# Routing in a mixture-of-experts stage: token weights formed later, column comparisons split per tile, placing matmuls dealt out between wide ones

## The reference

```
scores = sigmoid(x @ gate_w.T) + bias
topk_w, topk_idx = top_k(scores, 4)
topk_w = topk_w / (sum(topk_w) + 1e-20)
out = sum over the 4 chosen experts e of topk_w * (silu(x @ Wg[e].T) * (x @ Wu[e].T)) @ Wd[e].T
out = out + (silu(x @ Sg.T) * (x @ Su.T)) @ Sd.T      # the shared expert
x = layernorm(x + out)
```

## Time and profile before

| | us |
|---|---|
| median of 3 runs | 1754.04 (1752.56 to 1755.8) |
| profiled execution, its own time | 1757.54 |
| span of its trace | 1755.7 |
| PE busy | 1689.7 |
| DVE busy | 1267.1 |
| ACT busy | 919.4 |
| POOL busy | 958.2 |

### The profile page before, as it was taken

The page is one execution under the profiler, slowest core; times in us unless marked ns, Lnnn a source line. Parts: engine busy times, 40 slices in busy tenths (PEclk is TensorE's granted clock), DMA queues, the critical chain, the costliest instruction groups (busy, mean ns, idle before and its releaser), DMA issues. The chain is left out here.

```text
span 1755.7 us, 39041 instructions
## 1 busy us (share of the span) xinstructions
PE 1689.7 (96%) x15461; PEld 964.6 (55%) x15461; DVE 1267.1 (72%) x2051; ACT 919.4 (52%) x1518; POOL 958.2 (55%) x875
## 2 busy tenths in 40 slices
PE   7899998899999999999999999999899999999997
PEld 4666664455555555555555555555455555455553
DVE  6778776778888888888888888888785444344445
ACT  6776674656464645455555545565643333233334
POOL 5556664556464636465555555464634555455544
PEclk9999999899999999999999999999999999999999
DMA  5431223112212314122222122131266778877658
GB/s 163 133 86 39 74 62 80 61 58 88 70 64 72 109 43 142 46 100 93 72 73 97 37 97 73 37 109 37 77 226 216 145 146 224 241 190 151 116 97 299
DMA packets 88897, 190.68 MB, mean 109 GB/s; under 512 B 14800, under 2 KB 33744, under 8 KB 86672
## 3 DMA queue, kind: packets, MB, share of 16 engines
q1 hardware_dynamic: 65232, 130.72, 22.3%
q0 software_dynamic: 22912, 57.32, 16.0%
q10 hardware_dynamic: 576, 0.14, 0.0%
HBM read 124.95 MB, written 63.21 MB: 107 GB/s over the span
## 5 line engine op out<-in xcount | busy, mean ns | idle before, releaser
L1136 POOL TENSOR_TENSOR xa_sc<-xa_sc,xa_rs 128x1024 f32<-128x1024 f32 x32 | 60.8, 1901 | 375.4 <-DVE xa_rs L1396 375.4
L1125 POOL TENSOR_TENSOR xa_xs<-xa_xs,sn 128x512 f32<-128x512 f32 x160 | 233.7, 1460 | 46.3 <-ACT xa_xs L1177 46.3
L288 PE MATMUL bank<-xhl,front_h 128*128 128x512 f16 x640 | 244.4, 382 | 11.3 <-DVE front_l L670 10.0
L289 PE MATMUL bank<-xhl,front_h 128*128 128x512 f16 x640 | 244.3, 382 | 0.0
L290 PE MATMUL bank<-xhl,front_l 128*128 128x512 f16 x640 | 244.1, 381 | 0.0
L1130 POOL TENSOR_TENSOR xa_rr<-xa_x,xa_xs 128x512 f32<-128x512 f32 x160 | 232.2, 1451 | 12.7 <-DVE xa_x L1287 0.2
L2042 POOL DMA_INDIRECT scratch_y<-raw_front,moe_to x79 | 125.3, 1585 | 149.5 <-DVE mo_zl L2096 121.5
L288 PE MATMUL bank<-out_h,xa_oh 128*128 128x512 f16 x512 | 194.8, 381 | 10.2 <-DVE xa_ol L1269 8.0
L289 PE MATMUL bank<-out_l,xa_oh 128*128 128x512 f16 x512 | 194.7, 380 | 0.0
L290 PE MATMUL bank<-out_h,xa_ol 128*128 128x512 f16 x512 | 194.5, 380 | 0.0
L1176 ACT ACTIVATE xa_xs<-bank 64x512 f32<-64x512 f32 x160 | 95.0, 593 | 139.3 <-PE bank L290 124.4
(11 more groups left out here) (320 smaller groups left out, 4668.8 us busy)
## 6 DMA issues: line engine op xcount, KB each, us to landing
xa_rawc<-in_ew SPq DMA_DIRECT2D x32, 768.0 KB, 5.4
moe_ring<-scratch_w SPq DMA_DIRECT2D x16, 1536.0 KB
scratch_w<-xa_chunk_h SPq DMA_DIRECT2D x32, 384.0 KB, 2.3
scratch_w<-xa_chunk_l SPq DMA_DIRECT2D x32, 384.0 KB, 3.3
raw_front<-in_xwq SPq DMA_DIRECT2D x8, 1024.0 KB, 7.9
raw_out<-in_xwo SPq DMA_DIRECT2D x8, 1024.0 KB, 5.3
scratch_y<-acc SPq DMA_DIRECT2D x6, 1024.0 KB, 7.8
acc<-in_x POOLq DMA_DIRECT2D x4, 1024.0 KB, 7.2
```

Source lines behind the costliest of these rows:

```text
L288: pe.matmul(out_ap, ah, bh, start=start and m == 0, stop=False)
L289: pe.matmul(out_ap, ah, bl, start=False, stop=False)
L1125: PO.mark(pool.tensor_tensor(xr, xr, sn[:, :].rearrange("p (a s) -> p a s", a=1) .to_broadcast([P, QT // S, S]), ALU.mult), f"sm{r}", st)
L1136: PO.mark(pool.tensor_tensor(s4, s4, rs[:, :, :].rearrange("p h (t a) -> p (h t) a", a=1) .to_broadcast([P, 16, S]), ALU.mult), "nm", st)
```

## The change

It does four things.

**Column comparisons.** `hit` and its semaphore are gone. Where DVE made a group's `at_col` with two operations over 128x664 (a comparison with the column numbers, then a product with the token numbers), it now makes it with eight operations over 128x83, each a comparison and a product in one, whose two scalars are read per partition (`colf[:, j, t:t+1]` and `m.tok_no[:, t:t+1]`). `at_col` is laid out [P, 8, 83] in place of [P, 83, 8], so that a placing matmul streams 83 adjacent elements; `at_row` keeps its layout, its 128 weights 16 bytes apart. The float16 copy `col` goes, a float16 copy `ioh` of the column numbers is made ahead of the scores.

**Tokens' weights.** The four operations that make `m.w4` move from ahead of the counts to behind `locate(0, 1, 2, 3)`.

**Placing matmuls.** 24 of groups 0 to 3 follow a wide matmul of gu1.1 each and the other 8 stand behind it; 12 of groups 4 to 7 follow a wide matmul of y0.2 and y0.3 each, and the other 20 stand behind. y0.0 and y0.1 move ahead of gu1.1.

**Low part.** zl of the quarter q = 1 moves from POOL to DVE, behind "list", and PE waits for it there.

```diff
-            at_row, at_col = ([b(f"{w}{n}", [P, c, NR], F16) for n in range(NB)] for w, c in (("at_row", P), ("at_col", COLS)))
-            hit, s_hit = [b(f"hit{n}", [P, COLS, NR], F16) for n in range(2)], sem("ro_hit")
+            at_row, at_col = ([b(f"{w}{n}", shape, F16) for n in range(NB)] for w, shape in (("at_row", [P, P, NR]), ("at_col", [P, NR, COLS])))
+            ioh = b("ioh", [P, P], F16)
...
             PE = Timeline(sem("ro_pe"), [], 0,
-                          ["logits"] + quad("gu", 0, IB) + ["counts"] + quad("gu", 1, IB) + several("place", *range(4)) + ["y0.0"]
-                          + several("place", *range(4, 8)) + ["owners", "y0.1", "y0.2", "y0.3", "y1.0", "y1.1", "turn0", "y1.2", "turn1", "y1.3"])
+                          ["logits"] + quad("gu", 0, IB) + ["counts", "gu1.0", "y0.0", "y0.1", "place0", "place1", "gu1.1", "place2", "place3", "y0.2", "place4",
+                                                                "y0.3"] + several("place", *range(5, 8)) + ["owners", "y1.0", "y1.1", "turn0", "y1.2", "turn1", "y1.3"])
...
-                          ["down", "chosen"] + quad("z", 0, IB) + ["w4", "slots"] + several("at", *range(4)) + quad("z", 1, IB)
-                          + several("at", *range(4, 8)) + ["own", "list", "tables", "to", "xl0", "xl1", "ws0", "ws1"])
+                          ["down", "chosen"] + quad("z", 0, IB) + ["slots"] + several("at", *range(4)) + ["w4"] + quad("z", 1, IB)
+                          + several("at", *range(4, 8)) + ["own", "list"] + quad("zl", 1, IB) + ["tables", "to", "xl0", "xl1", "ws0", "ws1"])
...
-                        dve.tensor_tensor(hit[g % 2][:, :, :], io8[:, 0:COLS, :], along(col[:, j, ts], COLS), ALU.is_equal).then_inc(s_hit, 1)
                         dve.tensor_tensor(at_row[g % NB][:, :, :], io8[:, :, :], along(row[:, j, ts], P), ALU.is_equal)
-                        dve.wait_ge(s_hit, g + 1)
-                        i = dve.tensor_tensor(at_col[g % NB][:, :, :], hit[g % 2][:, :, :], along(m.tok_no_h[:, ts], COLS), ALU.mult)
+                        for n in range(NR):
+                            t = ts.start + n
+                            i = dve.tensor_scalar(at_col[g % NB][:, n, :], ioh[:, 0:COLS], colf[:, j, t:t + 1], m.tok_no[:, t:t + 1],
+                                                  ALU.is_equal, ALU.mult)
...
                 products(0)
-                then(dve.tensor_reduce(tot[:, :], top8[:, :, 0:TOPK], AX.X, ALU.add))
...
                 wait(dve, PE, "counts")
...
                 locate(0, 1, 2, 3)
+                then(dve.tensor_reduce(tot[:, :], top8[:, :, 0:TOPK], AX.X, ALU.add))
...
                 products(1)
                 locate(4, 5, 6, 7)
...
+                for n in range(IB):
+                    wait(dve, AC, f"zh1.{n}")
+                    DV.mark(dve.tensor_tensor(zl[1][:, n, :], z[:, n, :], zh[1][:, n, :], ALU.subtract), f"zl1.{n}", N0)
...
-                front(1)
-                place_picks(0, 1, 2, 3)
-                back(0, 0)
-                place_picks(4, 5, 6, 7)
+                front(1, 0)
+                back(0, 0, 1)
+                front_with_places(1, 1, range(4))
+                back(0, 2, 3, groups=range(4, 8))
                 wait(pe, DV, "own")
                 PE.mark(pe.matmul(bank[1][0:1, 0:NTILES + 2], own_h[:, :], identh[:, 0:NTILES + 2], start=True, stop=True), "owners", N0)
-                back(0, 1, 2, 3)
                 back(1, 0, 1)
```

More of the change, by code:

```diff
@@ L1879, in logits, with place @@
                     return mm
-                def place_picks(*groups):
-                    for g in groups:
+                def place(g, n):
+                    if n == 0:
                         wait(pe, DV, f"at{g}")
[L1884 to L1888, removed]
+                    j, t = g * NR // NT, (g * NR + n) % NT
+                    mm = pe.matmul(bank[0][:, j * COLS:(j + 1) * COLS], at_row[g % NB][:, :, n], at_col[g % NB][:, n, :],
+                                   start=t == 0, stop=t == NT - 1, skip_group_check=True)
+                    if n == NR - 1:
@@ L1889, in place_picks, with front @@
                         PE.mark(mm, f"place{g}", N0)
-                def front(q, ns=range(IB)):
+                def front(q, n):
                     tok = slice(q * QT, (q + 1) * QT)
[L1893 to L1901, removed]
@@ L1903, in back @@
-                def back(q, *ts):
+                    if q:
+                        wait(pe, DV, f"z{q - 1}.{n}")
+                    for u in range(2):
+                        c = u * FI + n * P
+                        mm = three_pass(pe, bank[2 + 2 * n + u][:, :], [(wf_h[:, k, c:c + P], wf_l[:, k, c:c + P], xh[:, k, tok], xl[:, k, tok])
+                                                                       for k in range(KD)])
+                    PE.mark(mm, f"gu{q}.{n}", N0)
+                def places(groups, first, last):
+                    for m in range(first, min(last, NR * len(groups))):
+                        place(groups[m // NR], m % NR)
@@ new lines, in front_with_places @@
+                def front_with_places(q, n, groups):
+                    wait(pe, DV, f"z{q - 1}.{n}")
+                    tok, m = slice(q * QT, (q + 1) * QT), 0
+                    for u in range(2):
+                        c, o = u * FI + n * P, bank[2 + 2 * n + u]
+                        for k in range(KD):
+                            h, l = wf_h[:, k, c:c + P], wf_l[:, k, c:c + P]
+                            for w, x in ((h, xh), (l, xh), (h, xl)):
+                                mm = pe.matmul(o[:, :], w, x[:, k, tok], start=k == 0 and w is h and x is xh,
+                                               stop=k == KD - 1 and x is xl, skip_group_check=True)
+                                m += 1
+                                if m == 6 * KD:
+                                    PE.mark(mm, f"gu{q}.{n}", N0)
+                                places(groups, m - 1, m)
+                    places(groups, m, 4 * NR)
@@ L1904, in back @@
+                def back(q, *ts, groups=()):
                     if q == 0:
                         wait(pe, DV, "down")
-                    wait(pe, PO, f"zl{q}.1")
+                    wait(pe, DV if q else PO, f"zl{q}.1")
+                    m = 0
                     for t in ts:
```

33 lines of the change are left out of this document (20 added, 13 removed).

## The result

The changed kernel takes 1760.25 us (median of 9 runs, 1758.24 to 1763.82) against 1755.12 (9 runs, 1752.03 to 1757.15) on the same chip: ratio 1.0032, 95% interval 1.0022 to 1.0041, so it is slower by 5.6 us (3.9 to 7.2 at the interval's ends). 4.1 us were forecast.

The account below looks back on a forecast made before the run. The prediction took SP's queue as the bound: the late write delays the fourth load and so turn0 by 4.1 us, added to the median 1754.04 for 1758.1 us. Range 1753.0 to 1761.0, its own 1756.9 to 1760.

Parts of the forecast that it names:

- Price of the new operation: DVE's groups: pitch p of one 83-value operation with two per-partition operands, 0.22 us, a group 2.36 us.
- Start of the groups: DVE behind the counts: the first group starts 1.27 us earlier, at 1315.05 instead of 1316.32.
- The write: SP's queue: the write of the tokens' weights is delayed by max(0, 32p - 2.93), 4.1 us at p = 0.22.
- the fourth load: SP's queue: the fourth expert's weights, behind the write, are issued at 1335.8 instead of 1331.68.
- Rows land with the fourth load.: DMA queues: the first gathered rows land as the fourth load ends, at 1343.2 in the changed kernel.
- Delay of turn0 = delay of the load.: Turning of the first gathered rows: comes 4.1 us later, at 1343.2 against 1339.1, nothing absorbing the delay.
- The later list is hidden; none of PE's order counts.: List about 7 us later, at 1338.5, hidden by the load; PE's 7 us saved in placing turn into waits.
- the 1 us of the forecast: PE before turn0: 12 wide matmuls of 0.216 take it to 1342.2, 1 us ahead of the rows.
- One operand's price: Rival on DVE's pitch: p about 0.16, write delayed 1.2 to 3.1 us, time 1755.3 to 1757.2; chance 0.27.
- free operands: Rival on DVE's pitch: p up to 0.11, delay up to 0.6 us, time 1754 to 1754.7; chance 0.12.
- "Faster": Rival: rows come before the fourth load, turn0 4 to 4.8 us earlier, time about 1749.5; chance 0.08.
- The forecast's other term for PE: PE before turn0: some 8 of 12 wide matmuls at half clock bring it to 1343.9, 0.7 us late.

Follow-up runs that it names:

- a4: Changed kernel with 24 more DVE operations of 83 float16 values behind the last table, results unused; its one time was 1761.61 us.
- a2: Changed kernel, but the write of the tokens' weights on SP's queue waits for at6 instead of w4; ratio to before 1.0047.
- b3: Changed kernel, but SP issues the fourth load only when the first gather's rows have landed; ratio to before 1.0033.
- c2: Kernel before, but SP issues the fourth load right behind the third without waiting for its landing; ratio to before 1.0002.
- a1: Changed kernel, but the write of the tokens' weights waits for the fifth group (at4) instead of w4; ratio to before 1.0031.
- a3: Changed kernel with the three operations per group and the at_col layout of before; ratio to before 1.0016.
- b1: Kernel before with only the changed kernel's column comparisons and at_col layout; ratio to before 1.0041.
- b2: Changed kernel with the weights' four operations back ahead of the counts; ratio to before 1.0042.
- c3: Kernel before, placing matmuls dealt out two behind each wide one of y0.0 to y0.3, fourth load issued right behind the third; ratio 1.0005.
- c4: Changed kernel with the three operations per group of before and the second quarter's low part back on POOL; ratio to before 1.0030.

## Why the prediction was right, and where not

- *Price of the new operation*, 0.22: measured 0.211, operands additive. Right. The size of VectorE's operand, 0.053 to 0.060, isn't the 93 ns that the Trainium skill's "ScalarE: Activation LUTs", section What ACT_TABLE_LOAD costs, gives for ScalarE. Nor do eight at 0.098 without such operands show the fixed 150 cycles per small tile of the Trainium skill's "VectorE: DVE Perf Modes", its section on the TRN2 errata; the measured pitch decides.
- *Start of the groups*, 1.27 us earlier: from the counts to the first group 8.56 us before and 7.35 now, 1.21 earlier. Right.
- *The write*, 4.1 later: 3.94; *the fourth load* 4.09. Right.
- *Rows land with the fourth load.* Shown by the landings in the changed kernel, a4 and a2, 0.5 to 0.7 us behind the load, and by a4 against b3: with the same list, turn0 is 2.0 us earlier when the load is issued behind the rows. For the kernel before it was too strong: c2 takes the load away and turn0 comes no earlier, so PE bound it there as well. The rule of the Trainium skill's "DMA: Bandwidth & Descriptors", section Queues, rings and completion order, under which a gather's packets take turns with the load's, is borne out only in a1, where the gather was issued first: there turn0 had its rows 5.0 us after the start of the load's issue, and that load landed after 8.1.
- *Delay of turn0 = delay of the load.* This is the term that was mis-sized: 5.56 for 4.1. The load was issued 4.09 later, and 8.9 us passed from there to turn0 where 7.5 did. Most of it is the load itself: its last packet ended 8.0 us after the start of its issue, and 7.0 in the kernel before. By the view of the DMA queues it landed after 8.5 us here, as in a3, and after 6.7 in b1 and 6.6 in b2 (the trace of before has no landing for it):

```profile
moe_ring<-scratch_w SPq DMA_DIRECT2D x1, 1536.0 KB, 8.5
```

  In the windows of the long ones (changed, a3, a4 with 8.3) the page of queues has one packet of the instruction queue q8 more, which those of b1 and b2 haven't:

```profile
q8 instruction: 1, 0.02, 0.7%
```

  That a fetch of instructions on one DMA engine holds up that engine's share of the load is what the packets say. In the changed kernel 127 of the load's 128 packets of 12 KB had started by 1339.5, the packet of q8 ran from 1339.56 to 1340.50, and the load's last one started at 1340.48:

```profile
q1 hardware_dynamic: 1, 0.01, 119.2%
```

  (the line of the load's queue in the view of 1340.45 to 1340.50; the share is over 100% because the packet outlasts the window). In a2, a3 and c3 too the load's last packet starts as q8's ends, 0.8 to 1.1 us behind the one before it; where no packet of q8 is about, that step is 0.6 us at most. The gathers that overlap a load may lengthen it besides: a1's fourth load took 8.1 us with no packet of q8 in its way. No run takes the one or the other away.
- *The later list is hidden; none of PE's order counts.* Right only in so far as the load stood in front. b3 takes the load away and is still 3.1 us late at turn0; b2 gives the early write back and gains nothing. The list was 5.65 us late, and behind it the low part (1.9 us of wait) and wide matmuls at half clock (12 of them, granted clock 0.50) took PE to turn0 at 36.0, 1 us before the rows. That PE was ahead by the 1 us of the forecast is luck: it came 1.5 us later than forecast (34.4), and so did the rows (36.9 for 35.4). With the load on time PE would have been the bound, 4.6 us later than in the kernel before. What I hadn't seen is that PE's order makes a chain of waits by itself (a3). In the changed kernel it is hidden, as DVE, busy from the counts to the last group, is no later for it.
- *Rivals.* One operand's price and free operands fall with a4. "Faster" fell: the list was too late, as forecast (64p against 32p). The forecast's other term for PE, up to 0.7 us behind rows at 35.4 if it ran at half clock, came true (0.5 behind), but the rows were later still.
- *Slips in the working.* The write's delay is 32p - 3.0 by the forecast's own figures, not 32p - 2.93, which makes 4.0 for 4.1. The range of p from 0.20 to 0.27 gives 1757.5 to 1759.8, or 1760.5 with PE late, and not 1756.9 to 1760. The "faster" rival adds 3.9 us behind the groups where the forecast's list has 4.6. None of them moves a result across a line.

## What to carry to other kernels

Where an engine is always busy and yet another chain ends at the same moment, delaying either costs in full or nearly so (the load by 4.1 us: 5.6; the list by 7.6: 6.9), and speeding up one is worth nothing where it was tried (the load, in c2): look for what ends last at the joint, and for how close the second is. Before small work is dealt out between large pieces, follow who waits for the large piece: its end moves by all that is put inside. And eight operations of 83 numbers with two per-partition operands cost 1.69 us where two of 664 cost 0.83.

## What was not expected of the hardware

- A gather of 128 rows, free of loads, landed 3.5 us after the start of its issue (b1) and was used after 3.7 (c3); behind a load of 1.5 MB in flight it landed after 5.9 (a2) to 6.6 (a4). Its packets didn't take turns with those of a load that was issued before it: the first went as the first DMA engine was done with its part of the load.
- One packet of 16 KB of instructions, some 0.95 us on one DMA engine, ends just as the last packet of a load starts in four traces (changed, a2, a3, c3), 0.8 to 1.1 us behind the other packets.
- POOL's two-tensor operation of 512 float32 numbers stretched float16 two-tensor operations of DVE from 0.49 and 0.68 us to 1.47 and 1.64 (c4), where beside the same work of POOL in the kernel before they ran at 0.50 and 0.68 and POOL took 7.73 us for two instead of 2.53.
- A stage that is shorter than the changed kernel's by 2.5 us (b3) or 1.8 (a3) gave nothing and 2.8 us in the time (ratios 1.0033 and 1.0016 against 1.0032; the intervals of the last two just overlap). In b3 the experts' loop behind it lost 1.5 us at one later gather; which gathers meet which loads there is not settled by these runs.
